# Attention block of a float32 macaron layer: the exponentials of the third query tile transposed by the DRAM exchange instead of by TensorE

## The reference, cut to what matters

```python
q = _rope(q.reshape(b, s, H, DQK).transpose(0, 2, 1, 3))
k = _rope(k.reshape(b, s, H, DQK).transpose(0, 2, 1, 3))
scores = jnp.einsum('bhqd,bhkd->bhqk', q, k) * (1.0 / np.sqrt(DQK))
scores = jnp.where(causal[None, None], scores, -jnp.inf)
probs = jax.nn.softmax(scores, axis=-1)
out = jnp.einsum('bhqk,bhkd->bhqd', probs, v)
out = out.transpose(0, 2, 1, 3).reshape(b, s, H * DV)
return out @ Wo + bo
```

## Time and profile before

| what | value |
|---|---|
| median of 3 runs | 2478.35 us (2475.99 to 2479.8) |
| the profiled execution's own time | 2474.15 us |
| its span, first to last instruction | 2471.0 us |
| TensorE busy | 2318.7 us, 94% |
| VectorE busy | 1866.0 us, 76% |
| ScalarE busy | 1462.3 us, 59% |
| GpSimd busy | 1500.2 us, 61% |
| mean granted TensorE clock | 0.985 |

### The profile page before, as it was taken

The page is one execution under the profiler, slowest core; times in us unless marked ns, Lnnn a source line. Parts: engine busy times, 40 slices in busy tenths (PEclk is TensorE's granted clock), DMA queues, the critical chain, the costliest instruction groups (busy, mean ns, idle before and its releaser), DMA issues. The chain is left out here.

```text
span 2471.0 us, 55023 instructions
## 1 busy us (share of the span) xinstructions
PE 2318.7 (94%) x17368; PEld 1805.3 (73%) x17368; DVE 1866.0 (76%) x3256; ACT 1462.3 (59%) x3741; POOL 1500.2 (61%) x1268
## 2 busy tenths in 40 slices
PE   7987899799999999999999999999999979986998
PEld 5763577578888888888788888888888856743676
DVE  6752377589888888888798898898898857731576
ACT  2321344377777787777777777777777743321343
POOL 1100345488888888887788888888888911100442
PEclk9999999999999999999999999999999989998999
DMA  8379654356666666566566566666666646579443
GB/s 257 120 260 380 257 177 153 103 155 182 174 175 172 172 180 177 161 180 172 157 185 170 162 185 171 171 177 169 185 170 165 181 119 235 200 270 381 141 151 106
DMA packets 340246, 460.87 MB, mean 187 GB/s; under 512 B 63616, under 2 KB 274176, under 8 KB 338944
## 3 DMA queue, kind: packets, MB, share of 16 engines
q1 hardware_dynamic: 339968, 457.47, 61.1%
HBM read 279.09 MB, written 111.15 MB: 158 GB/s over the span
## 5 line engine op out<-in xcount | busy, mean ns | idle before, releaser
L1435 POOL TENSOR_TENSOR att_z_sb<-att_z_sb,att_cos 128x512 f32<-128x512 f32 x255 | 360.2, 1413 | 197.4 <-DMA att_zs<-att_z_sb 197.0
L1438 POOL TENSOR_TENSOR att_z_sb<-att_z_sb,att_zs 128x512 f32<-128x512 f32 x255 | 362.9, 1423 | 20.0
L1436 POOL TENSOR_TENSOR att_zs<-att_zs,att_sin 128x512 f32<-128x512 f32 x255 | 357.1, 1400 | 0.0
L1645 ACT ACTIVATE att_last<-att_ps_w,att_nmax 128x512 f32<-128x512 f32 x256 | 173.5, 683 | 222.5 <-DVE att_nmax L1532 195.4
L1645 ACT ACTIVATE att_prob<-att_ps_x,att_nmax 128x384 f32<-128x384 f32 (+1 forms) x512 | 236.3, 482 | 0.0
L1818 PE MATMUL att_ps_p<-att_probT,att_v_sb 128*64 128x384 f32 (+2 forms) x1536 | 195.8, 390 | 6.6 <-DVE att_lastT L1550 6.5
L1443 POOL TENSOR_TENSOR att_kT_lo<-att_z_sb,att_kT_hi 128x512 fp32r<-128x512 f32 x128 | 163.5, 1277 | 31.9 <-ACT att_kT_hi L1631 31.9
L1055 POOL TENSOR_TENSOR com_b_kblk<-sh_blkmask,sh_kT 128x128 f32<-128x128 f32 x64 | 32.3, 525 | 242.7 <-POOLq L500 195.3
L1660 ACT COPY att_probT<-att_ps_p 128x512 f32<-128x512 f32 x256 | 151.3, 591 | 43.6 <-PE att_ps_p L1804 38.0
L1818 PEld LDWEIGHTS att_ps_p<-att_probT,att_v_sb 128*64 128x64 f32 x1536 | 100.5, 137 | 102.8 <-issue 83.0
L180 POOL TENSOR_SCALAR dis_b_veps<-dis_b_mv 128x4 f32<-128x4 f32 x31 | 13.3, 430 | 259.4 <-DVE dis_b_mv L174 259.4
(11 more groups left out here) (246 smaller groups left out, 7280.9 us busy)
## 6 DMA issues: line engine op xcount, KB each, us to landing
att_zs<-att_z_sb SPq DMA_DIRECT2D x512, 128.0 KB, 2.4
last_tile_blocks<-att_last SPq DMA_DIRECT2D x128, 512.0 KB, 3.5
att_got<-last_tile_blocks SPq DMA_DIRECT2D x512, 128.0 KB, 2.9
att_R<-inverse_sums SPq DMA_DIRECT2D x256, 128.0 KB, 4.3
ffn_w<-in_e_W SPq DMA_DIRECT2D x30, 1024.0 KB, 9.5
ffn_wg<-in_e_Wg SPq DMA_DIRECT2D x24, 1024.0 KB, 13.0
x_normalised_transposed<-dis_b_xnT SPq DMA_DIRECT2D x32, 512.0 KB, 3.0
ffn_w<-in_e_W SPq DMA_DIRECT2D x32, 512.0 KB, 15.8
```

The costliest lines, as they stand in the source:

```text
L1435: nc.gpsimd.tensor_tensor(z[:, m, i, :], z[:, m, i, :], cos[:], ALU.mult)
L1436: nc.gpsimd.tensor_tensor(zs[:, m, i, :], zs[:, m, i, :], sin[:], ALU.mult).then_inc(sin_s[i].sem, 1)
L1438: nc.gpsimd.tensor_tensor(z[:, m, i, :], z[:, m, i, :], zs[:, m, i, :], ALU.add).then_inc(sum_s[i].sem, 1)
L1645: nc.scalar.activation(dst, src, ACT.Exp, bias=nmax[:, p % 2, qt, hh:hh + 1], accum_out=sums[:, p % 2, hh, qt:qt + 1]).then_inc(exp_s.sem, 1)
```

## The change

Tile 2 joins tile 3 on the way through DRAM. `put` and `get` move 1792 columns instead of 1024, and so does VectorE's `turn`. TensorE turns the three blocks a head of tiles 0 and 1: group 0 is four blocks, group 1 is two, and both go into `ps_p`; ScalarE copies both, and VectorE's `copy_pt` and its semaphore are gone. `mix` has two key blocks in its wide part and fourteen matmuls of 128 columns in the other. `exps` of tile 2 takes the place of that of tile 1 and the other way round; `largest(SPLIT)` takes the place of `largest(MIDDLE)` and the other way round. `copy_pt` 0 stands behind the high part of the query. `put` waits for the exponentials of both tiles. `result` writes `acc` throughout and `xout` is gone; the wait for the store of the sequence before moves from the last part of the sum to the first.

```diff
-    LAST, QB = TT - 1, P // QUAD
+    NEAR, QB = TT - 2, P // QUAD
+    FAR = {TT - 1: 0, TT - 2: TT}
+    NF = 2 * TT - 1
-    TURNS = (None, ((0, 0), (0, 2)), ((1, 0), (1, 2)), ((0, 1), (1, 1)))
+    TURNS = [[(hh, kb) for hh in range(2)] for kb in range(NEAR)]
-    WIDE, MIDDLE, SPLIT = range(3)
-    MAX_AT = (4, 2, 4, 1)
+    WIDE, SPLIT, MIDDLE = range(3)
+    MAX_AT = (3, 4, 3, 1)
...
# SyncE: put, and the store of the sequence before
-                need_held(sp, exp_s, j, 8 * u + 2)
+                need_held(sp, exp_s, j, 8 * u + 4)
...
-                    sp.dma_start(tiles(out_dram, j - 1), xout[:]).then_inc(out_s.sem, 16)
+                    sp.dma_start(tiles(out_dram, j - 1), acc[:]).then_inc(out_s.sem, 16)
...
# VectorE: result
                 if grp % 4 == 0:
                     dve.wait_ge(xb_s.sem, xb_s.at(j, TT * (w // NP + 1)))
-                if grp % 4 == 3:
                     dve.wait_ge(out_s.sem, out_s.at(j, 16 * (w // NP)))
...
# VectorE: copy_pt is taken out, turn and slot
-                nc.vector.transpose(lastT[:].rearrange("p a (t r) -> p t a r", r=QUAD), got[:]).then_inc(turn_s.sem, 1)
+                nc.vector.transpose(farT[:].rearrange("p a (t r) -> p t a r", r=QUAD), got[:]).then_inc(turn_s.sem, 1)
...
                 if t.has(p):
-                    largest(j, p, MIDDLE)
+                    largest(j, p, SPLIT)
                 if t.has(p - 2):
                     divide(j, p - 2)
-                if t.has(p - 1):
-                    copy_pt(j, p - 1, 1)
                 if t.has(p):
-                    largest(j, p, SPLIT)
+                    largest(j, p, MIDDLE)
...
# ScalarE: copy_pt and slot
-                act.wait_ge(pt_mm.sem, pt_mm.at(j, 3 * p + k))
-                a = OFF[TURNS[k][0]]
-                nc.scalar.copy(probT[:, a:a + S], turn_bank(k)[:]).then_inc(pta_s.sem, 1)
+                act.wait_ge(pt_mm.sem, pt_mm.at(j, NEAR * p + k + 1))
+                nc.scalar.copy(probT[:, START[k]:START[k + 1]], mix_bank[:, 0:START[k + 1] - START[k]]).then_inc(pta_s.sem, 1)
...
                 if t.has(p):
-                    exps(j, p, 1)
+                    exps(j, p, 2)
                 if t.has(p - 2):
                     high_part(j, p - 2)
-                if t.has(p - 1):
-                    copy_pt(j, p - 1, 2)
                 if t.has(p + 1):
                     high(j, p + 1, 0)
+                if t.has(p - 1):
+                    copy_pt(j, p - 1, 0)
                 for u in t.values()[0:1]:
                     values(j, u)
                 if t.has(p - 1):
-                    copy_pt(j, p - 1, 3)
+                    copy_pt(j, p - 1, 1)
...
                 if t.has(p):
-                    exps(j, p, 2)
+                    exps(j, p, 1)
                     exps(j, p, 0)
...
# TensorE: transposes (group 1 waits for the copy of group 0) and slot
-                    pe.wait_ge(pta_s.sem, pta_s.at(j, 2 * p + 1))
+                    pe.wait_ge(pta_s.sem, pta_s.at(j, NEAR * p + 1))
...
+                for u in first_value:
+                    for half in range(2):
+                        values(t, u, half)
                 if turned:
+                    transposes(t, 0)
+                if turned and p == X_TURN:
                     transposes(t, 1)
-                for u in first_value:
-                    values(t, u, 0)
-                if turned:
-                    transposes(t, 2)
-                for u in first_value:
-                    values(t, u, 1)
-                if turned and p == X_TURN:
-                    transposes(t, 3)
...
                 if out:
                     output(t, p - OUT0, 0)
                 if turned and p != X_TURN:
-                    transposes(t, 3)
+                    transposes(t, 1)
                 if out:
                     output(t, p - OUT0, 1)
```

More of the change, by code:

```diff
@@ L1231, in attention_phase @@
     NP = PAIRS
-    LAST, QB = TT - 1, P // QUAD
-    WIDTH = [LAST * P - kb * P for kb in range(LAST)]
+    NEAR, QB = TT - 2, P // QUAD
+    FAR = {TT - 1: 0, TT - 2: TT}
+    NF = 2 * TT - 1
+    WIDTH = [NEAR * P - kb * P for kb in range(NEAR)]
     OFF = {}
-    TURNS = (None, ((0, 0), (0, 2)), ((1, 0), (1, 2)), ((0, 1), (1, 1)))
-    at = 0
-    for turn in TURNS[1:]:
+    TURNS = [[(hh, kb) for hh in range(2)] for kb in range(NEAR)]
+    START, at = [], 0
+    for turn in TURNS:
+        START.append(at)
         for hk in turn:
@@ L1319, in attention_phase @@
         masked = sb("masked", [P, P], BF16)
-        acc, xout = (sb(x, [P, TT, D]) for x in ("acc", "xout"))
+        acc = sb("acc", [P, TT, D])
         stats, mv, veps, rstd, shift = sb("st", [P, TT, 6]), sb("mv", [P, TT, 2]), sb("ve", [P, TT]), sb("rs", [P, TT]), sb("shift", [P, TT])
@@ L1633, in exps @@
             def exps(j, p, qt):
-                if qt == LAST:
+                if qt in FAR:
                     need(act, put_s, j, 16 * (p - 1))
                 else:
-                    need(act, pt_mm, j, 3 * (p - 1))
+                    need(act, pt_mm, j, NEAR * (p - 1))
                 need(act, inv_s, j, 2 * (p - 1))
@@ L1640, in exps @@
                 for hh in range(2):
-                    dst, src = prob[:, p % 2, hh, PLACE[qt]] if qt < LAST else None, scores_of(qt)[:, hh, :]
-                    if qt == LAST:
-                        dst = last[:, p % 2, :, hh].rearrange("p b k c -> p k b c")
+                    src = scores_of(qt)[:, hh, :]
+                    if qt not in FAR:
+                        dst = prob[:, p % 2, hh, PLACE[qt]]
+                    else:
+                        dst = far[:, p % 2, :, hh, FAR[qt]:FAR[qt] + qt + 1].rearrange("p b k c -> p k b c")
                         src = src.rearrange("p (k b c) -> p k b c", b=QB, c=QUAD)
@@ L1736, in project @@
                         need(pe, z_s[1], j, u)
-                    if t.first or t.p == LEAD:
-                        need(pe, ptv_s, j, u - 3)
                 w = (wq, wk)[i]
@@ L1787, in transposes @@
                 j, p = t.j, t.p - 1
-                if k == 1:
+                if k == 0:
                     if not t.has(t.p):
                         pe.wait_ge(exp_s.sem, exp_s.at(j, 8 * t.p))
-                    if t.has(p + 3):
-                        pe.wait_ge(z_s[1].sem, z_s[1].at(j, p + 4))
-                    elif p == X_TURN:
-                        pe.wait_ge(v_s.sem, v_s.at(j, NP))
-                    else:
-                        pe.wait_ge(xo_s.sem, xo_s.at(j, p + 1 - OUT0))
-                elif k == 2:
                     need(pe, on_s, j, p)
                 else:
-                    pe.wait_ge(pta_s.sem, pta_s.at(j, 2 * p + 1))
+                    pe.wait_ge(pta_s.sem, pta_s.at(j, NEAR * p + 1))
                 at = 0
                 for hh, kb in TURNS[k]:
-                    for qt in range(kb, LAST):
-                        last = nc.tensor.transpose(turn_bank(k)[:, at:at + P], prob[:, p % 2, hh, PLACE[qt]][:, kb * P:(kb + 1) * P], g.ident[:])
+                    for qt in range(kb, NEAR):
+                        last = nc.tensor.transpose(mix_bank[:, at:at + P], prob[:, p % 2, hh, PLACE[qt]][:, kb * P:(kb + 1) * P], g.ident[:])
                         at += P
@@ L1815, in mix @@
                 values_of = lambda kb, hh: v[:, (p // 2) % 2, kb, (p % 2) * P + hh * ADH:(p % 2) * P + (hh + 1) * ADH]
-                for kb in range(LAST):
+                for kb in range(NEAR):
                     for hh in range(2):
-                        nc.tensor.matmul(mix_bank[of_head(hh), kb * P:LAST * P], values_of(kb, hh), probT[:, OFF[hh, kb]:OFF[hh, kb] + WIDTH[kb]],
-                                         start=(kb == 0), stop=(kb == LAST - 1))
-                for kb in range(TT):
-                    for hh in range(2):
-                        last = nc.tensor.matmul(mix_bank[of_head(hh), LAST * P:S], values_of(kb, hh), lastT[:, hh * TT + kb, :],
-                                                start=(kb == 0), stop=(kb == TT - 1))
+                        nc.tensor.matmul(mix_bank[of_head(hh), kb * P:NEAR * P], values_of(kb, hh), probT[:, OFF[hh, kb]:OFF[hh, kb] + WIDTH[kb]],
+                                         start=(kb == 0), stop=(kb == NEAR - 1))
+                for qt, at in sorted(FAR.items()):
+                    for kb in range(qt + 1):
+                        for hh in range(2):
+                            last = nc.tensor.matmul(mix_bank[of_head(hh), qt * P:(qt + 1) * P], values_of(kb, hh), farT[:, hh * NF + at + kb, :],
+                                                    start=(kb == 0), stop=(kb == qt))
                 last.then_inc(pv_mm.sem, 1)
```

45 lines of the change are left out of this document (19 added, 26 removed).

## The result

| | before | changed |
|---|---|---|
| median of the runs beside each other | 2477.49 us | 2629.51 us |
| lowest to highest | 2475.99 to 2479.8 | 2626.16 to 2633.58 |
| the profiled execution | 2474.15 us | 2631.95 us |

The change made the kernel slower: ratio 1.0613, 95% interval 1.0593 to 1.0634. The forecast was 2591 us, in a range of 2535 to 2630. The direction and the wait ahead of transposes 1 came out as forecast; the size, 152 us, is more than the 113 of the sum, and the median lies 0.5 us inside the edge of the range. That it is inside is luck, as the upper end was made of other terms.

A forecast was written before the change was run, and what follows sets the result against it. TensorE, busy 98%, bounded a normal slot; after the change a closed chain of waits and VectorE's path would. A sequence of 102.25 us against 95.2, +7.05 times 16, gave +113 us: 2587 profiled, 2591 median, range 2535 to 2630.

The forecast's parts named there:

- the wait ahead of transposes 1: TensorE, before its second group of transposes: stands still about 1.0 us a slot until ScalarE has copied the first group.
- the upper end: 2630 us: VectorE's `turn` at 2.05 us and always contended, and the read back 0.2 late, 0.3 a slot.
- TensorE's saving: Six fewer transposes and a reshaped mix: net 0.48 us a slot, 61 us over 128 slots, if TensorE stays the bound.
- The chain: Cycle through TensorE, VectorE and ScalarE in program order: transposes 1 start at 6.9, a lap of 12.07 us against 11.48.
- Slot 5: Transposes 1 again at 6.9, then 9.17 less 0.18 to slot 6's zero: 15.9 us.
- VectorE's path: VectorE's `result` at 8.08, then `low_part` 1.12 and `turn` 1.96: sum 11.8, a normal slot 12.15 us in the mean.
- slots 6 and 0 to 2: Slot 6 with `query_low` behind `result` 12.8 us; slot 0 as a normal slot 12.15; slots 1 and 2 with statistics 12.45.
- covered, barely: Read back 1.75 times as large: there between 7.7 and 9.85 after the slot's zero, VectorE's `turn` at 9.8, so no cost.
- Priced at nothing: No cost for ScalarE's smaller copy, `put` waiting for tile 2's exponentials, the spread behind it, the `acc` store, the read back.
- TensorE stays the bound: Rival, at transposes 1: copy done by 5.9 after zero, slot 11.0, kernel 61 us faster, 2417 us; chance 0.08.
- The read back becomes the bound: Rival, ahead of VectorE's `turn`: data land at 11.0, slots end at 13.0, +189, 2667 us; chance 0.07.
- The Trainium skill's rule: Pointed to the rival that VectorE's work alone counts: 0.19 us a slot more, +24 us, 2503 us; chance 0.03.

The follow-up runs named there:

- query_turn: Changed kernel with ScalarE's query cast ahead of tile 2's exponentials and TensorE's transposes 1 behind the second output half: 2561.61 us, ratio 1.0327.

## Why the prediction was right, and where the size was off

**TensorE's saving.** Right in a slot at the full clock. The mix takes 0.70 and 1.62 us (1221.36, 1222.06, 1223.68) for 0.68 and 1.70, transposes 0 0.41 and transposes 1 0.19. I could not know whether the saving would be worth its 61 us: with the bytes and the longer transpose gone, and the chain open but in slot 5, it was worth 20.

**The chain.** Right, each step within 0.04 us (its last sum is 12.06, not 12.07). That the order costs the time is shown by experiment: the order alone makes a loss of 133 us without any of the change's work, taking the exchange's work back leaves 98 us, and moving two items gives back 68. That the chain through ScalarE is all of it is not shown, as `divide` came later by the same order. And in most slots the lap closed through VectorE's own path (12.15 in the forecast, 12.54 in the slot shown), as the sum allowed for.

**Slot 5.** Right: 15.86 us between the last two lines of the next fence, for 15.9.

**VectorE's path, and slots 6 and 0 to 2.** The direction was right. Its transpose takes 2037 ns in the median for 2021 reckoned. But the slots came out longer. The zeros of slots 6 to 0 of one sequence, and those of slots 5 and 6 at its end:

```profile
984.92 0.43 DVE L1530 TENSOR_TENSOR att_ps_w<-att_ps_w,att_masked 128x256 f32<-128x256 f32 x1 [0.68 <-PE att_ps_w L1755]
...
999.21 0.39 DVE L1530 TENSOR_TENSOR att_ps_w<-att_ps_w,att_masked 128x256 f32<-128x256 f32 x1
1011.59 0.40 DVE L1530 TENSOR_TENSOR att_ps_w<-att_ps_w,att_masked 128x256 f32<-128x256 f32 x1
1024.49 0.40 DVE L1530 TENSOR_TENSOR att_ps_w<-att_ps_w,att_masked 128x256 f32<-128x256 f32 x1
...
1074.04 0.43 DVE L1530 TENSOR_TENSOR att_ps_w<-att_ps_w,att_masked 128x256 f32<-128x256 f32 x1
1089.90 0.43 DVE L1530 TENSOR_TENSOR att_ps_w<-att_ps_w,att_masked 128x256 f32<-128x256 f32 x1 [1.01 <-PE att_ps_w L1755]
```

Slot 6 took 14.29 for 12.8, slot 7 12.38 and slot 0 12.90 for 12.15. Over all sequences the medians were 13.57 for slot 6, 12.08 for slot 7, 12.52 for slot 0, 12.43 for slot 4 and 12.6 for slots 1 and 2, for which I had 12.45. Three terms of the sum were too small:

- *The read back, "covered, barely".* Of the three it has the highest price by experiment. I let landing end at 9.85 after zero and `turn` begin at 9.8, which is not a cover of 0.1, as I wrote, but a lack of 0.05. In the changed kernel VectorE waited for it 44 times, 31.5 us, and taking the bytes back gave 26. Its median landing went from 2.9 to 4.5 us, but the last of the four counts: in the slot shown their issue ended at 1225.42 and VectorE could begin at 1231.21, 5.8 us later, above the 5.1 that I had as the upper bound. In the next slot (zero 1233.18) the issue itself was late as well, because the rotation's exchange ahead of it on SyncE took longer:

```profile
1232.23 3.42 SPq L1368 DMA_DIRECT2D att_zs<-att_z_sb  x4
1235.91 0.36 SPq L1373 DMA_DIRECT2D inverse_sums<-att_rsumT  x1
1236.53 1.76 SPq L1393 DMA_DIRECT2D att_got<-last_tiles_blocks  x4
```

  It ended 5.1 after zero for 4.75. My upper end of the range had only 0.2 us a slot for all of that.
- *`low_part` in slot 6.* I put 1.12, the mean of an instruction that ran from 0.65 to 1.8 us. In slot 6 it took 1.77 or 1.78 us, 1.70 up to the next start, in 15 of 16 sequences. In the next slot 6, whose `result` came at 8.07 as forecast:

```profile
1099.82 1.77 DVE L1558 TENSOR_TENSOR att_oT_lo<-sh_kT,att_oT_hi 128x512 fp32r<-128x512 f32 x1
1101.51 2.03 DVE L1546 STREAM_TRANSPOSE att_farT<-att_got 128x1792 f32<-128x1792 f32 x1
```

  That is 0.58 of slot 6's excess in each sequence, and VectorE did not wait for the read back there. What slows the instruction no run tried.
- *The clock, which cost nothing in the kernel before.* See below; I had no term for it.

Of the 45 us between the reckoned 2587 and the profiled 2631.95, the bytes are 26 by experiment. The others are read from the trace, and with the 26 they add up to more than 45, so they don't split it: `low_part` in slot 6 about 9 us, the clock in slot 6 about 7, some 8 outside the stretch from the first mix to the last (158 less 149), and 8.6 in one slot 3 of 20.75 us (zeros at 1258.89 and 1279.64). In that slot TensorE stood still for 5.71 us with nothing that the profile shows as the cause. Every trace of this case has one such long slot 3 in the same sequence, also that of the kernel before, where it was 15.84 us and the longest such time ahead of TensorE's projections 2.7. That one stays open.

**Priced at nothing.** No compute engine waits for the store from `acc` or for the spread behind the later `put` in the profile after, nor for ScalarE's smaller copy, that of transposes 1. SyncE itself now waits ahead of `put` for ScalarE's exponentials, 69 times, 34.5 us. That was read, not tried by a run.

**The rivals.** *TensorE stays the bound* failed at its stated place, as the wait of transposes 1 is 0.94 us, above the 0.48 below which it would hold. *The read back becomes the bound* did not come true in the changed kernel, but it does in `query_turn`, where the chain no longer hides it. The Trainium skill's rule (Perfetto Trace Analysis, Identifying the Most-Contended Engine) pointed at VectorE when TensorE is judged by its weight loads; the section names the matmul work done against the peak beside them, which I left out. It was halfway right, as taking 0.79 us off VectorE gave 28 us with the chain closed, but 98 us of the loss stayed with that work taken back.

## What to carry to other kernels

Where engines run in program order and wait for each other in a ring, follow one lap of the ring by hand before moving work: take each engine's instructions in their order, with durations from the timeline, until you are back where you began. If the lap is longer than the fullest engine's work, taking work off that engine buys nothing unless it shortens the lap, and a change of order can cost more than the work saved. And read what is queued behind a small transfer as well as ahead of it, since moving a big one in front delays everybody who waits for the small one.

## What the runs showed of the hardware that I had not expected

TensorE's clock fell within slot 6. Before the change it was granted in full over the whole stretch. The windows of one slot 6 after (columns as above), and at the end one of the next slot 6:

```profile
989.60:991.80 2.20, 1.36 (x10) 1.16 (x10) 1.00 (x2) 2.15 (x6) 2.12 (x3) 1.00 1.06 235
991.80:993.80 2.00, 2.00 (x9) 2.00 (x10) 0.03 (x1) 1.31 (x6) 2.00 (x3) 0.52 1.10 290
993.80:996.00 2.20, 2.20 (x8) 1.68 (x8) 2.20 (x3) 0.74 (x5) 2.12 (x3) 0.66 0.95 360
...
1096.80:1098.80 2.00, 2.00 (x13) 1.82 (x14) 0.83 (x2) 1.54 (x8) 2.00 (x2) 1.00 1.06 245
```

and what TensorE did before it:

```profile
989.62 0.66 PE L1788 MATMUL att_ps_p<-sh_ident,att_prob 128*128 128x128 f32 x4 [1.54 <-DVE sh_kT L1553]
...
991.80 0.64 PE L1788 MATMUL att_ps_p<-sh_ident,att_prob 128*128 128x128 f32 x2 [0.82 <-ACT att_probT L1655]
```

It had stood still for 1.54 us and, 1.4 us later, for 0.82; then the granted clock was 0.52, the lower of its two levels (1.2 of 2.4 GHz) nearly throughout. Two transposes took 0.64 us for 0.44 in the normal slot above, `result` came at 8.85 after zero for 8.08, and that is half of slot 6's excess. The next slot 6 had idle times at the same places and kept the full clock, so not each of them pays. Of the 16 slots 6, six had a granted clock of 0.50 to 0.57 in these two us, and they lasted 14.29 to 14.39 us; nine had 1.00 and lasted 12.95 to 13.70, with a median of 13.16. So a fall costs about 1.1 us. What decides which slots pay, no run here shows.

The long slot 3 has a fall too. Behind its 5.71 us of idle time:

```profile
1272.60:1278.00 5.40, 5.40 (x12) 3.78 (x12) 0.00 (x0) 0.69 (x1) 0.89 (x1) 0.50 0.06 19
```

A pair of its projections took 1.05 us there, for 0.62 in a normal slot. The Trainium skill (TensorE: Matmul & The Clock Gate, The HAM clock gate) says that the clock falls when TensorE has been idle. The rows of this slot and of six slots 6 agree; the nine others, with idle times as long, show that being idle for so long is not enough by itself. A new idle time on the engine that had none can cost more than its own length.
